# Two of down's four block copies go from VectorE to ScalarE, and tile 14's product is split around the turns of tile 15

## The chip, the cores and the metric

The kernel runs on one core of one Trainium2 chip. The metric is the device time of one launch in microseconds (us), the median of several runs. Its span is the time from the first to the last instruction in a profiled execution.

## The reference

`x` is 64 x 32 x 512 (batch, head, position). First a long convolution per head: a kernel `K` of 512 taps is made from state-space parameters and convolved causally with `x`, masked by a length per batch entry. The result goes through a feed-forward block with ternary weights:

```python
xq = int4_quant(x)                       # round(x * sqrt(7) / mean|x|), clipped to -8..7, rescaled
gate = bitlinear(xq, w_gate, s_gate)     # w_q = clip(round(w / mean|w|), -1, 1)
up = bitlinear(xq, w_up, s_up)
gate = jnp.square(jax.nn.relu(gate))
inter = int8_quant(up * gate)            # round(x * 127 / max|x|)
return bitlinear(inter, w_down, s_down)  # 1376 -> 512
```

The output is `x` plus that. `w_gate` and `w_up` are 1376 x 512, `w_down` is 512 x 1376.

## The kernel before

The 2048 rows are cut into T = 16 tiles of 128 rows (two heads by 64 batch entries). Each engine has its own program, written out by hand, and semaphores tie them together. A loop over slots m = 0..15 runs on every engine; slot m computes the `gate` and `up` products of tile m in three chunks of columns (416, 512, 448; c = 0, 1, 2), and works on other tiles beside them.

TensorE in slot m: `products(m, 0)`, the turns of x for tile m + 4 (`xt`), `products(m, 1)`, `products(m, 2)`, `down` of one or two older tiles (`DOWNS`: none up to slot 4, tile 0 in slot 5, tiles 11 and 12 in slot 14, tile 13 in slot 15), and `conv(m + 4)`. `gate_ps` and `up_ps` have two banks each, so an `up` product waits until the `inter` of two chunks before is made. After slot 15 come `turn_last` (eleven turns of tile 15's rounded `inter` into two PSUM banks), `down(14)` and `last_down`, tile 15's product in two halves of 256 columns.

ScalarE in slot m: `relu_square(c)` for each chunk, two instructions (L780, L783); between them the absolute sum of a later tile (`y_sum`), the copy of the turned x (`xt_copy`), and `y_round(m + 2)` (L745), directly ahead of `relu_square(2)`. It is called by VectorE's `y_scale(m + 2)`. In slot 4 an x load (`load_half(act, 4, 1)`, L347) follows `relu_square(2)`.

VectorE in slot m: `gated(c)` for each chunk, which makes `inter` from `up_ps` and ScalarE's `g2` (L1114) and takes its maximum (L1118); then the row's scale, the rounding of `inter` (L1161), the cast of a turned `inter` (`i_cast`, L1091), the output of older tiles (`out_add`, L1097) and the mask of a `conv` (`y_mask`, L1037). Between `gated(0)` and `gated(1)` stand `q_copy` and `y_scale`.

The weights of down are rounded in slot 2 into `w_int[2]`, turned in four blocks of 128 output columns by DMA transposes that SP issues (`turn_down(0)` and `(1)` in its slot 2, `(2)` and `(3)` in its slot 3, L411) into `dn_turned`, and `down_copy(k)` (L1024) clips block k, 128 x 1408 int16, to -1..1 and writes it as bf16 into `down_t`. VectorE does all four copies in slot 4 (LAG is 5): blocks 0 and 1 ahead of `gated(1)`, blocks 2 and 3 behind it. `down(0)` in slot 5 is the first reader of `down_t`.

At the end VectorE rounds the first 896 columns of tile 15's `inter` and ScalarE the other 480 (L816); both cast the turns. ScalarE also casts tile 14's turned `inter` (L814). `half_add(0)` and `half_add(1)` (L1104) write tile 15's output into `o_sb[1]`, which held tile 13's output, so they wait for tile 13's two stores. SP stores half 0 and ScalarE's queue half 1.

Of the kernel before, what the change touches and what calls it, by code (L numbers as in the profile page):

```python
# [5 lines left out]
P = 128  # L6
ALU = mybir.AluOpType
ACT = mybir.ActivationFunctionType
# [15 lines left out]
def adaln_ffn(nc, x, length, log_dt, C, log_A_real, A_imag, Dskip,  # L24
              w_gate, w_up, w_down, s_gate, s_up, s_down, out):
    B, H, L = x.shape
# [3 lines left out]
    T = B * H // P  # L30
    KB = L // P
    IB = -(-I // P)
# [14 lines left out]
    LAG = 5  # L47
# [8 lines left out]
    with ExitStack() as ctx:  # L56
# [6 lines left out]
        def sem(name):  # L63
            return ctx.enter_context(nc.semaphore(name))

        gate_ps = [psum("gate_ps0"), psum("gate_ps1")]
# [62 lines left out]
        c1 = sb("c1", [P, 2, HG])  # L129
# [95 lines left out]
        w_act_copied = sem("w_act_copied")  # L225
        down_turned = [sem(f"down_turned{k}") for k in range(KB)]
        down_copied = sem("down_copied")

        xt_turned = sem("xt_turned")
        xt_copied = sem("xt_copied")  # L230
# [39 lines left out]
        def half_rows(half):  # L270
            return slice(half * B, (half + 1) * B)
# [79 lines left out]
        def _(sp):  # L351
# [88 lines left out]
            sp.wait_ge(half_ready, 1)  # L440
            for half in range(2):
                sp.dma_start(out[:, head_of(T - 1, half), 0:L // 2],
                             o_sb[1][half_rows(half), 0:L // 2]).then_inc(half_stored[0], 16)
            sp.wait_ge(stored[0], 32 * (T // 2))
            sp.wait_ge(stored[1], 32 * (T // 2 - 1))
            sp.wait_ge(half_stored[0], 32)
# [48 lines left out]
        def _(pe):  # L495
# [25 lines left out]
            def conv(n):  # L521
                pe.wait_ge(xt_copied, n + 1)
                pe.wait_ge(toep_loaded[n % 4], 16 * (n // 4 + 1))
                wait(pe, y_masked, n - 1)
                if n == 1:
                    pe.wait_ge(winv_ready, 2)
                if n == EARLY + 3:
                    pe.wait_ge(k_ready, 3)
                bank = conv_bank(n)
                for i in range(KB):  # L530
                    for half in range(2):
                        mm = pe.matmul(bank[half * B:(half + 1) * B, 0:L - i * P],  # L532
                                       x_t[n % 2][:, i, half * B:(half + 1) * B], toep[n % 4][:, half, i * P:L],
                                       start=(i == 0), stop=(i == KB - 1))
                mm.then_inc(conv_done, 1)
# [85 lines left out]
            def turn_last():  # L621
                pe.wait_ge(inter_quant, T)
                for c in range(IT_SPLIT):
                    mm = pe.transpose(tr_act_ps[:, c * P // 2:(c + 1) * P // 2].bitcast(BF16),
                                      inter_q[:, c * P:(c + 1) * P].bitcast(BF16), ident_bf[:])
                mm.then_inc(it_turned, 1)
                pe.wait_ge(last_quant, 1)
                for c in range(IT_SPLIT, IB):
                    r = P if c < WIDE else IR
                    o = (c - IT_SPLIT) * P // 2  # L630
                    mm = pe.transpose(tr_dve_ps[0:r, o:o + P // 2].bitcast(BF16),
                                      inter_q[:, c * P:c * P + r].bitcast(BF16), ident_bf[:])
                mm.then_inc(it_turned, 1)

            def down(n):
                if n == T - 2:
                    pe.wait_ge(it_act_copied, 1)
                else:
                    pe.wait_ge(it_copied, n + 1)
                if n == 0:  # L640
                    pe.wait_ge(down_copied, KB)
                if n == 8:
                    pe.wait_ge(y_masked, T)
                if down_before(n) is not None:
                    pe.wait_ge(out_ready, down_before(n) + 1)
                bank = down_bank(n)
                for c in range(IB):
                    r = P if c < WIDE else IR
                    mm = pe.matmul(bank[:], i_t[n % 2][0:r, c, :], down_t[0:r, c, :],  # L649
                                   start=(c == 0), stop=(c == IB - 1))  # L650
                mm.then_inc(down_done, 1)

            def last_down():
                pe.wait_ge(it_copied, T - 1)
# [10 lines left out]
            for m in range(T):  # L665
                products(m, 0)
                if m > 0 and m + EARLY < T:
                    xt(m + EARLY)
                products(m, 1)
                if m == 0:  # L670
                    xt(3)
                    conv(2)
                    first_q(1)
                if m == 1:
                    k_sums(2)
                if m == 2:
                    mean(2)
                products(m, 2)
                if m == 0:
                    xt(EARLY)  # L680
                    conv(3)
                for n in DOWNS[m]:
                    if n < T - 2:
                        down(n)
                if m + EARLY < T:
                    conv(m + EARLY)
            turn_last()
            down(T - 2)
            last_down()

        @block.scalar
        def _(act):
# [32 lines left out]
            def weight_copy(i):  # L725
                act.wait_ge(w_turned, i + 1)
                dst, src = inner_blocks(i)
                nc.scalar.activation(dst, src, ACT.Sign).then_inc(w_act_copied, 1)

            def xt_copy(n):  # L730
                act.wait_ge(xt_turned, n + 1)
# [7 lines left out]
            def y_round(n):  # L739
                act.wait_ge(yscale_ready, n + 1)  # L740
                if n >= 4:
                    act.wait_ge(q_loaded[n % 2], 16 * (n // 2 - 1))
                elif n >= 2:
                    act.wait_ge(q_turned, n - 1)
                nc.scalar.activation(y_int[n % 2][:], y[n % 3][:], ACT.Copy, scale=yscale[n % 2][:]  # L745
                                     ).then_inc(y_rounded, 1)
# [27 lines left out]
            for m in range(T):  # L774
                def relu_square(c):
                    cn = CH[c][1]
                    bank = (NC * m + c) % 2
                    act.wait_ge(gate_done, NC * m + c + 1)
                    wait(act, inter_ready, NC * m + c - 1)
                    nc.scalar.activation(g2[bank][:, 0:cn], gate_ps[bank][:, 0:cn], ACT.Relu,  # L780
                                         scale=gu_scale[m % 4][:, 0:1]).then_inc(relu_done, 1)
                    act.wait_ge(relu_done, NC * m + c + 1)
                    nc.scalar.activation(g2[bank][:, 0:cn], g2[bank][:, 0:cn],  # L783
                                         ACT.Square).then_inc(g2_ready, 1)

                relu_square(0)
                if 1 <= m < T - 2:
                    y_sum(m + 2)
                relu_square(1)
                if m == 0:  # L790
                    xt_copy(3)
                    load_half(act, 3, 1)
                    y_sum(2)
                elif m + EARLY < T:
                    xt_copy(m + EARLY)
                if 1 <= m < T - 2:
                    y_round(m + 2)
                relu_square(2)
                if m == 0:
                    y_round(2)  # L800
                    xt_copy(EARLY)
                if m == 4:
                    for i in range(2):
                        act.wait_ge(w_rounded[2][i], rounds(2, i))
                    load_half(act, 4, 1)
                if m < 2:
                    act.wait_ge(w_turned, len(TURNS))
                    weight_sum(2, m)
                if m == 2:
                    down_round(2)  # L810
                    down_round(3)
# [13 lines left out]
            act.wait_ge(half_ready, 2)  # L825
            for half in range(2):
                act.dma_start(out[:, head_of(T - 1, half), L // 2:L],
                              o_sb[1][half_rows(half), L // 2:L]).then_inc(half_stored[1], 16)

        @block.vector  # L830
        def _(dve):
# [268 lines left out]
            def half_add(half):  # L1100
                cols = slice(half * L // 2, (half + 1) * L // 2)
                dve.wait_ge(half_done, half + 1)
                dve.wait_ge(stored[1], 32 * (T // 2 - 1))
                v.scalar_tensor_tensor(out=o_sb[1][:, cols], in0=gate_ps[half][:, 0:L // 2],  # L1104
                                       scalar=oscale[:, T - 1:T], in1=x_tile(T - 1)[:, cols],
                                       op0=ALU.mult, op1=ALU.add).then_inc(half_ready, 1)

            for m in range(T):
# [15 lines left out]
                    q_copy(m + 1)  # L1124
                if 1 <= m < T - 2:
                    y_scale(m + 2)
                if m == LAG - 1:
                    down_copy(0)
                    down_copy(1)
                gated(1)  # L1130
                if m == 0:
                    y_mask(2)
                    q_copy(1)
                    y_scale(2)
                if m == LAG - 1:
                    down_copy(2)
                    down_copy(3)
                if m == 1:
                    k_copy(2)
                    dve.wait_ge(w_turned, len(TURNS))  # L1140
# [70 lines left out]
```

## Time and profile before

| | us |
|---|---|
| timed runs | 209.33, 212.88, 214.0 |
| median | 212.88 |
| the profiled execution, its own time | 208.22 |
| span of the profiled execution | 206.4 |
| TensorE busy in the span | 174.8 |
| VectorE busy | 159.3 |
| ScalarE busy | 114.2 |

The times of the rows below are from the profiled execution, counted from the start of its span. PE is TensorE, DVE is VectorE, ACT is ScalarE, SPq and ACTq are the queues on which SP and ScalarE issue DMAs. The program's names come without their numbers: `inter<-up_ps,gu_scale,g` is L1114. `x4` is the number of instructions merged into one row. `L1114` is line 1114 of the kernel. An entry in brackets at a row's end is how long the engine had been idle before it and what released it. Slot 3 is about 73 to 81 us on TensorE and 77 to 85 us on VectorE, slot 4 81 to 89 and 85 to 95, slot 5 starts at 89 on TensorE.

### The profile page before, as it was taken

How to read it: one execution, taken by the hardware profiler on the slowest of the kernel's cores; microseconds unless marked ns; L12 is line 12 of the kernel's file. 1: busy time of each engine (PE TensorE's matmuls, PEld its weight loads, DVE VectorE, ACT ScalarE, POOL GpSimd, SP SyncE). 2: the span in 40 equal slices, each digit the busy share in tenths (PEclk: the TensorE clock that was granted, in tenths of full speed). 3: DMA queues.
4: the chain of work that ended last, by engine and by line, in shares of the span. 5: the costliest groups of instructions: out<-in, count | busy, mean ns of one | idle time of the engine just before them, and what ended most of it. 6: DMA issues, size and time to landing. Idle time of an engine off the chain costs nothing.

```text
span 206.4 us, 3336 instructions
## 1 busy us (share of the span) xinstructions
PE 174.8 (85%) x1059; PEld 92.7 (45%) x1075; DVE 159.3 (77%) x425; ACT 114.2 (55%) x191; POOL 28.4 (14%) x71
## 2 busy tenths in 40 slices
PE   1003599895999999995999999999999999999982
PEld 1003476652464554452545454545454544444451
DVE  6999495567167898999877787878787989897851
ACT  2363685656478995863382736364554628162720
POOL 5024998950000000000000000000000000000000
PEclk9999999998899999999999999999999999999999
DMA  4999499999934487999575554747471618274424
GB/s 138 362 366 317 74 262 350 398 221 223 191 76 115 97 210 151 243 190 254 153 139 149 111 158 94 176 94 171 99 171 37 122 25 173 44 155 80 92 54 102
DMA packets 49487, 34.25 MB, mean 166 GB/s; under 512 B 37598, under 2 KB 37886, under 8 KB 49470
## 3 DMA queue, kind: packets, MB, share of 16 engines
q1 hardware_dynamic: 45502, 25.65, 54.1%
q10 hardware_dynamic: 3968, 8.39, 13.1%
q8 instruction: 9, 0.15, 0.3%
q14 instruction: 8, 0.07, 0.1%
HBM read 21.07 MB, written 4.28 MB: 123 GB/s over the span
## 4 chain that ended last, share of the span: by engine, by line
PE 66%; DMA 14%; DVE 9%; ACT 4%; issue 3%; POOL 1%; SPq 1%; DVEq 0%; POOLq 0%; ACTq 0%
PE gate_ps L612 14%; PE up_ps L617 13%; PE down_ps L649 11%; DMA raw<-in_L_ffn_w_up_dram 8%; PE conv_ps L532 6%; PE tr_dve_ps L532 6%; DMA raw<-in_x_dram 5%; PE conv_ps L649 5%; PE down_ps L532 4%; PE tr_act_ps L518 3%; DVE inter L1114 2%; ACT int L710 2%; DVE y L1037 1%; DVE imax L1118 1%; ACT g L780 1%
## 5 line engine op out<-in xcount | busy, mean ns | idle before, releaser
L780 ACT ACTIVATE g<-gate_ps,gu_scale 128x416 f32<-128x416 f32 (+2 forms) x48 | 30.6, 637 | 52.9 <-PE gate_ps L612 52.6
L1114 DVE SCALAR_TENSOR_TENSOR inter<-up_ps,gu_scale,g 128x416 f32<-128x416 f32 (+2 forms) x48 | 33.3, 693 | 20.9 <-ACT g L783 20.6
L617 PE MATMUL up_ps<-up_t,q_t 128*128 128x512 bf16 (+2 forms) x190 | 44.6, 357 | 2.9 <-DVE inter L1114 2.8
L612 PE MATMUL gate_ps<-gate_t,q_t 128*128 128x448 bf16 (+2 forms) x181 | 42.8, 356 | 0.6
L1118 DVE TENSOR_REDUCE imax<-inter 128x1 f32<-128x416 f32 (+2 forms) x48 | 30.3, 631 | 1.7
L783 ACT ACTIVATE g<-g 128x416 f32<-128x416 f32 (+2 forms) x48 | 28.1, 585 | 1.5
L617 PEld LDWEIGHTS up_ps<-up_t,q_t 128*128 128x128 bf16 x192 | 18.5, 98 | 21.9 <-DVE inter L1114 4.1
L649 PE MATMUL down_ps<-down_t,i_t 128*128 128x512 bf16 (+1 forms) x119 | 27.7, 379 | 0.1
L612 PEld LDWEIGHTS gate_ps<-gate_t,q_t 128*128 128x128 bf16 x192 | 17.7, 98 | 16.0 <-issue 2.1
L710 ACT ACTIVATE int<-raw 128x2048 bf16<-128x2048 f32 (+3 forms) x8 | 15.6, 1944 | 9.3 <-DMA raw<-in_L_ffn_w_gate_dram 5.2
L532 PE MATMUL conv_ps<-toep,x_t 128*64 128x512 f32 (+3 forms) x128 | 19.0, 439 | 0.0
L649 PEld LDWEIGHTS down_ps<-down_t,i_t 128*128 128x128 bf16 (+1 forms) x121 | 11.8, 98 | 13.7
L745 ACT ACTIVATE y_int<-y,yscale 128x512 int16<-128x512 f32 x16 | 11.5, 721 | 6.0 <-DVE yscale L1045 5.7
L1161 DVE TENSOR_SCALAR inter_q<-inter,iscale 128x1376 int16<-128x1376 f32 x15 | 14.0, 936 | 0.5
L532 PEld LDWEIGHTS conv_ps<-toep,x_t 128*64 128x64 f32 x128 | 8.7, 136 | 11.2 <-issue 9.8
L737 ACT ACTIVATE y_abs<-y 128x512 bf16<-128x512 f32 x16 | 9.9, 616 | 5.5 <-DVE y L1037 5.5
L509 PE MATMUL down_ps<-wsum,averaging 128*128 128x3 f32 (+1 forms) x6 | 1.5, 312 | 12.9 <-ACT int L710 12.9
L532 PE MATMUL tr_dve_ps<-toep,x_t 128*64 128x512 f32 (+3 forms) x80 | 11.9, 439 | 0.0
L733 ACT COPY x_t<-tr_act_ps 128x512 f32<-128x512 f32 x16 | 9.2, 574 | 3.5 <-PE tr_act_ps L518 3.5
L649 PE MATMUL conv_ps<-down_t,i_t 128*128 128x512 bf16 (+1 forms) x44 | 10.2, 379 | 0.0
L518 PE MATMUL tr_act_ps<-ident,raw 128*128 128x128 f32 x48 | 7.7, 285 | 2.2 <-DMA raw<-in_x_dram 2.2
L1037 DVE SCALAR_TENSOR_TENSOR y<-steps,lens,conv_ps 128x512 f32<-128x512 f32 x8 | 5.9, 742 | 3.7 <-PE conv_ps L532 3.7
(179 smaller groups left out, 206.0 us busy)
## 6 DMA issues: line engine op xcount, KB each, us to landing
toep<-k_back SPq DMA_DIRECT2D x16, 512.0 KB, 4.1
out_dram<-o_sb SPq DMA_DIRECT2D x30, 128.0 KB, 2.4
raw<-in_x_dram ACTq DMA_DIRECT2D x3, 512.0 KB, 8.5
raw<-in_x_dram SPq DMA_DIRECT2D x3, 512.0 KB, 9.5
raw<-in_L_ffn_w_down_dram ACTq DMA_DIRECT2D x1, 1472.0 KB, 14.7
raw<-in_L_ffn_w_down_dram ACTq DMA_DIRECT2D x1, 1280.0 KB, 9.4
raw<-in_L_ffn_w_gate_dram ACTq DMA_DIRECT2D x1, 1024.0 KB, 5.6
raw<-in_L_ffn_w_gate_dram SPq DMA_DIRECT2D x1, 1024.0 KB, 10.4
```

Source lines behind the costliest of these rows:

```text
L518: mm = pe.transpose(tr_act_ps[:, i * P:(i + 1) * P], x_tile(n)[:, i * P:(i + 1) * P], ident[:])
L532: mm = pe.matmul(bank[half * B:(half + 1) * B, 0:L - i * P], x_t[n % 2][:, i, half * B:(half + 1) * B], toep[n % 4][:, half, i * P:L], sta ...
L612: mm = pe.matmul(gate_ps[bank][:, 0:cn], q_t[m % 3][:, i, :], gate_t[:, i, c0:c0 + cn], start=(i == 0), stop=(i == KB - 1))
L617: mm = pe.matmul(up_ps[bank][:, 0:cn], q_t[m % 3][:, i, :], up_t[:, i, c0:c0 + cn], start=(i == 0), stop=(i == KB - 1))
L649: mm = pe.matmul(bank[:], i_t[n % 2][0:r, c, :], down_t[0:r, c, :], start=(c == 0), stop=(c == IB - 1))
L710: nc.scalar.activation(w_bits[m][weight_part(m, i)], raw[m][weight_part(m, i)], ACT.Abs, accum_out=wsum[:, m, i:i + 1]).then_inc(w_summed, 1)
L745: nc.scalar.activation(y_int[n % 2][:], y[n % 3][:], ACT.Copy, scale=yscale[n % 2][:]).then_inc(y_rounded, 1)
L780: nc.scalar.activation(g2[bank][:, 0:cn], gate_ps[bank][:, 0:cn], ACT.Relu, scale=gu_scale[m % 4][:, 0:1]).then_inc(relu_done, 1)
L783: nc.scalar.activation(g2[bank][:, 0:cn], g2[bank][:, 0:cn], ACT.Square).then_inc(g2_ready, 1)
L1114: v.scalar_tensor_tensor(out=inter[:, c0:c0 + cn], in0=up_ps[bank][:, 0:cn], scalar=gu_scale[m % 4][:, 1:2], in1=g2[bank][:, 0:cn], op0=AL ...
L1118: return v.tensor_reduce(imax[:, c:c + 1], inter[:, c0:c0 + cn], AX.X, ALU.max, apply_absolute_value=True)
L1161: v.tensor_scalar(inter_q[:, 0:I], inter[:], iscale[:], None, ALU.mult).then_inc(inter_quant, 1)
```

## The change

Block 1 of down is copied by ScalarE in slot 3 and block 3 by ScalarE in slot 4, each between `y_round` and `relu_square(2)`, by an activation `Sign` (the values are whole numbers, so it is the clip). VectorE copies block 0 in slot 3 and block 2 in slot 4, both between `gated(1)` and `gated(2)`. `down(0)` waits for two copies of each engine. `down(14)` is cut: its first four matmuls stand ahead of `turn_last`, the other seven behind it. Tile 15's output goes into the first 512 columns of `inter` instead of `o_sb[1]`, and `half_add` no longer waits for tile 13's stores.

```diff
+        down_act_copied = sem("down_act_copied")
             for half in range(2):
                 sp.dma_start(out[:, head_of(T - 1, half), 0:L // 2],
-                             o_sb[1][half_rows(half), 0:L // 2]).then_inc(half_stored[0], 16)
+                             inter[half_rows(half), 0:L // 2]).then_inc(half_stored[0], 16)
...
-            def down(n):
+            def down(n, c0=0, c1=IB):
...
                 if n == 0:
-                    pe.wait_ge(down_copied, KB)
+                    pe.wait_ge(down_copied, KB // 2)
+                    pe.wait_ge(down_act_copied, KB // 2)
...
-                for c in range(IB):
+                for c in range(c0, c1):
...
-                mm.then_inc(down_done, 1)
+                if c1 == IB:
+                    mm.then_inc(down_done, 1)
...
+            down(T - 2, 0, 4)
             turn_last()
-            down(T - 2)
+            down(T - 2, 4)
             last_down()
...
+            def down_copy(k):
+                act.wait_ge(down_turned[k], 16)
+                nc.scalar.activation(down_t[:, :, k * P:(k + 1) * P], dn_turned[:, k],
+                                     ACT.Sign).then_inc(down_act_copied, 1)
...
                 if 1 <= m < T - 2:
                     y_round(m + 2)
+                if m in (3, 4):
+                    down_copy(2 * m - 5)
                 relu_square(2)
...
                 act.dma_start(out[:, head_of(T - 1, half), L // 2:L],
-                              o_sb[1][half_rows(half), L // 2:L]).then_inc(half_stored[1], 16)
+                              inter[half_rows(half), L // 2:L]).then_inc(half_stored[1], 16)
...
                 dve.wait_ge(half_done, half + 1)
-                dve.wait_ge(stored[1], 32 * (T // 2 - 1))
-                v.scalar_tensor_tensor(out=o_sb[1][:, cols], in0=gate_ps[half][:, 0:L // 2],
+                v.scalar_tensor_tensor(out=inter[:, cols], in0=gate_ps[half][:, 0:L // 2],
...
-                if m == LAG - 1:
-                    down_copy(0)
-                    down_copy(1)
                 gated(1)
...
-                if m == LAG - 1:
-                    down_copy(2)
-                    down_copy(3)
+                if m in (3, 4):
+                    down_copy(2 * m - 6)
```

## Rows read from the trace of the kernel before

**Rows 1.** Windows of core 0: stretch, busy time (instructions) per engine, granted clock, DMA share.

```profile
50.00:54.00 4.00, 4.00 (x16) 1.71 (x17) 1.32 (x4) 2.91 (x3) 0.00 (x0) 0.59 1.40 195
95.83:100.00 4.17, 4.17 (x21) 1.75 (x23) 3.52 (x9) 1.82 (x3) 0.00 (x0) 1.00 0.92 168
100.00:196.00 96.00, 95.47 (x507) 46.77 (x513) 79.14 (x180) 49.91 (x91) 0.00 (x0) 1.00 0.52 118
```

**Rows 2.** Timeline of TensorE: start, length, instruction, [idle before and its releaser].

```profile
49.80 1.08 PE L518 MATMUL tr_act_ps<-ident,raw 128*128 128x128 f32 x4 [2.23 <-DMA raw<-in_x_dram]
50.81 3.58 PE L532 MATMUL down_ps<-toep,x_t 128*64 128x512 f32 x16
54.34 2.37 PE L532 MATMUL conv_ps<-toep,x_t 128*64 128x512 f32 x16
...
91.85 1.04 PE L617 MATMUL up_ps<-up_t,q_t 128*128 128x512 bf16 x4 [0.17 <-DVE inter L1114]
...
95.83 0.93 PE L617 MATMUL up_ps<-up_t,q_t 128*128 128x448 bf16 x4 [2.18 <-DVE inter L1114]
```

**Rows 3.** Chain that ended last, 86 to 91 us: start, length, what.

```profile
86.66 1.58 DVE down_t L1024 x2
...
90.33 0.88 DVE down_t L1024
```

**Rows 4.** Timeline of all engines, 194 to 203 us.

```profile
194.05 1.35 ACT L814 CAST i_t<-raw 128x1408 bf16<-128x1408 int16 x1
...
196.99 0.56 PE L624 MATMUL tr_act_ps<-ident_bf,inter_q 128*128 128x128 bf16 x7 [0.99 <-DVE inter_q L1165]
...
201.90 0.48 DVE L1104 SCALAR_TENSOR_TENSOR o_sb<-gate_ps,oscale,raw 128x256 f32<-128x256 f32 x1 [0.95 <-DMA out_dram<-o_sb]
...
202.60 0.48 DVE L1104 SCALAR_TENSOR_TENSOR o_sb<-gate_ps,oscale,raw 128x256 f32<-128x256 f32 x1 [0.22 <-PE gate_ps L661]
```

**Rows 5.** Chain that ended last, 197 to 203 us.

```profile
197.78 2.38 PE conv_ps L649 x11
200.16 2.42 PE gate_ps L661 x22
```

**Rows 6.** Instructions of line 728: count, shortest/median/longest ns, first and last start.

```profile
L728 ACT ACTIVATE gate_t<-up_ps x2: 1005/1009/1013, 28.6 to 35.4; 128x1024 bf16<-128x1024 int16 x2
```

**Rows 7.** Timeline of slots 3 and 4, VectorE, ScalarE and its queue.

```profile
79.33 0.72 ACT L745 ACTIVATE y_int<-y,yscale 128x512 int16<-128x512 f32 x1 [1.19 <-DVE yscale L1045]
...
79.96 0.62 ACT L780 ACTIVATE g<-gate_ps,gu_scale 128x448 f32<-128x448 f32 x1
79.98 0.69 DVE L1118 TENSOR_REDUCE imax<-inter 128x1 f32<-128x512 f32 x1
...
81.22 0.69 DVE L1114 SCALAR_TENSOR_TENSOR inter<-up_ps,gu_scale,g 128x448 f32<-128x448 f32 x1 [0.56 <-ACT g L783]
...
84.80 0.65 DVE L1114 SCALAR_TENSOR_TENSOR inter<-up_ps,gu_scale,g 128x416 f32<-128x416 f32 x1
...
86.70 0.72 ACT L745 ACTIVATE y_int<-y,yscale 128x512 int16<-128x512 f32 x1 [0.64 <-DVE yscale L1045]
...
88.03 0.63 ACTq L347 DMA_DIRECT2D raw<-in_x_dram  x1
...
91.12 0.68 DVE L1114 SCALAR_TENSOR_TENSOR inter<-up_ps,gu_scale,g 128x448 f32<-128x448 f32 x1
```

**Rows 8.** Line 411 by halves; then landing times of down's blocks 1, 2 and 3.

```profile
L411 SPq DMA_TRANSPOSE int<-int x2: 1747/1938/2128, 73.1 to 75.3; - x2
...
L411 SPq DMA_TRANSPOSE int<-int x2: 1392/2224/3056, 82.0 to 83.4; - x2
...
int<-int SPq DMA_TRANSPOSE x1, 4.0
...
int<-int SPq DMA_TRANSPOSE x1, 4.8
...
int<-int SPq DMA_TRANSPOSE x1, 6.2
```

## The prediction

> **What bounds the kernel now.** I read the windows first, because they say where TensorE has room. From 100 to 196 us it is busy for 95.47 of 96 us at full granted clock [rows 1]: nothing that happens on another engine there can move the end, and what TensorE loses before 100 us it never gets back. So two places count: what delays TensorE before that stretch, the four copies of down's turned blocks among it, and the tail behind 196 us.
>
> TensorE's own timeline shows its pauses in slots 4 and 5. The last `up` product of slot 5 starts at 95.83 after 2.18 us idle, the one before it at 91.85 after 0.17 us [rows 2]. Both wait for `inter` (L1114) on VectorE, since `up_ps` has two banks. Read next the chain of waits ahead of that product: `down_copy` stands on it, with 1.58 us for its first two and 0.88 us for its last [rows 3]. VectorE is the bound of slot 4, the four copies being 3.2 us of it (4 x 0.79).
>
> The tail is a line of dependent work: the seven turns of tile 15 begin at 196.99 after TensorE stood idle 0.99 us for VectorE's rounding, then come tile 14's eleven matmuls (2.38 us) and the 22 half matmuls (2.42 us) [rows 4, 5], `half_add(1)` at 202.60 [rows 4], and the last two stores, issued by ScalarE's queue.
>
> **The tail, part by part.** Four of tile 14's eleven matmuls move ahead of the turns: 4 x 2.38 / 11 = 0.87 us. They need `i_t[0]`, which ScalarE's cast gives at 194.05 + 1.35 = 195.40 [rows 4], and the output of tile 12 added, which VectorE does ahead of all its work of slot 15. TensorE falls idle at 196.00 and is called at 196.99, so 0.87 fits into 0.99 us, with 0.12 us over; bound of the price if the pipeline is slower to drain: 0 to 0.1 us. Behind the turns only 7 x 0.216 = 1.51 us remain, and they still cover the casts of tile 15: the turns end at 197.78 and the seven matmuls at 199.29, while the casts, of 896 columns and of 480, can't take longer than the 1.35 us of the 1408 above, which is 199.1. The half matmuls start 0.87 us earlier, at 199.29, and end at 201.71; `half_add(1)` starts at about 201.73 instead of 202.60.
>
> That only holds because of the buffer. Today `half_add(0)` waits 0.95 us for the store of tile 13 and starts at 201.90; it costs nothing, since `half_add(1)` waits for TensorE 0.22 us more after it [rows 4]. With the split alone, that store would still hold `half_add(0)` until 201.90 and `half_add(1)` would follow at 202.31, so the split would bring 0.3 us. With `inter` as target the wait is gone: `half_add(0)` can go at 199.29 + 1.21 = 200.5 plus the matmul's drain, in time behind tile 14's addition, which can start at 199.3. The two parts together give 0.87 us; all DMAs behind (SP's two for half 0, ScalarE's two for half 1) keep their number and size and move forward. `inter` is free: its last readers are the two roundings that the turns wait for. Bounds: 0.77 to 0.87 us gained.
>
> **The copies, part by part.** VectorE loses the four copies of slot 4 and gets one back in slot 3 and one in slot 4; one of its copies takes 0.88 us, 0.79 from start to start [rows 3]. ScalarE gets one in each slot. No `Sign` of this size is in the trace. Its cast of the same 1408 columns took 1.35 us [rows 4]; a `Sign` of 1024 columns out of PSUM took 1.01 us [rows 6], which scaled is 1.39. I take 1.35, or 1.26 from start to start, because instructions on ScalarE overlap by 0.09 us (`y_int` at 79.33 lasts 0.72 and its follower starts at 79.96 [rows 7]); bounds 1.2 and 1.4.
>
> What matters is where ScalarE's copy stands: between `y_round` and `relu_square(2)`, and `gated(2)` on VectorE waits for the latter. In slot 3 that is already the late side: `y_int` starts at 79.33, `gated(2)` at 81.22, after VectorE waited 0.56 us for ScalarE [rows 7]. So `gated(2)` goes to 81.22 + 1.26 = 82.48. VectorE's own copy is hidden there: `imax` at 79.98 ends at 80.67, the copy at 81.5. Price of slot 3: 1.26 us. Block 1, which ScalarE copies, is there: issued at 75.3, landed 4.0 us later [rows 8], 79.3, before ScalarE reaches it at 79.96.
>
> From `gated(2)` of slot 3 to `gated(0)` of slot 4 VectorE works without a stop, 84.80 - 81.22 = 3.58 us; new: 86.06. From there to slot 4's `y_int` 86.70 - 84.80 = 1.90 us [rows 7]: 87.96. Then ScalarE: the 1.89 us that slot 3 shows from `y_int` to `gated(2)`, and 1.26 for its copy, would let `gated(2)` start at 91.11. It started at 91.12 [rows 7]. So with all data there, what VectorE is rid of in slot 4 (three copies, 2.4 us) is spent exactly: ScalarE's copies stand on the path one after the other, and slots 3 and 4 together come out at nil. `gated(1)` and block 2's copy on VectorE (landed at 82.0 + 4.8 = 86.8 [rows 8]) end near 90.1 and are hidden.
>
> But block 3 is late. Its transpose is issued at 83.4 and lands 6.2 us later, at 89.6 [rows 8]. Before, `down_copy(3)` stood at 90.33 and did not see that. Now ScalarE would begin at 87.96 + 0.63 = 88.6 and waits 1.0 us, with `relu_square(2)` and the x load of the last quad queued behind it. SP issues the transpose behind the same things as before: its order is unchanged, and the `y_round` of slot 3 that it follows comes ahead of the first copy. So I keep 89.6. `gated(2)` of slot 4 starts at 92.15, 1.03 us later than now; VectorE works on without a stop to `gated(0)` of slot 5, which releases the product of 95.83. That product starts at 96.9. Bounds: with block 3 landed within the 4.0 us of block 1 (87.4) nil; with 7 us (90.4), +1.8.
>
> ScalarE's x load is issued at 88.03 today [rows 7], while block 3 is on its way. The Trainium skill (DMA: Bandwidth & Descriptors, section "Issuing engines are not separate DMA queues") says that DMAs of all issuing engines share the same 16 engines and interleave. By this rule the x load, now queued behind the copy, would leave block 3's last 1.6 us alone, and block 3 would land earlier by up to 1 us: the sum would be that of rival (a). No row of the trace shows a transpose with and without a load beside it, so it neither agrees nor disagrees.
>
> **The sum**, against the profiled execution (208.22 us, of which 206.4 span): -0.87 in the tail, +1.03 in slots 3 and 4 = +0.16 us, 208.4. The timed runs of before are 209.33, 212.88 and 214.0, and all four shown scatter over 5.8 us, far more than the change. Their middle is 211.1 with the profiled one and 212.88 without; I put the new median between, at 212.0 + 0.2 = 212.2 us. Two per cent, 4.3 us, is about what a measurement of this kernel can tell from no change.
>
> **Rivals.** (a) Block 3 lands by 88.6: slots 3 and 4 come out at nil, the tail's 0.87 us stands alone: profiled 207.35, median 211.2. For it: blocks 1 and 2 took 4.0 and 4.8 us. Against: SP's issue of one of the last two took 3.06 us where another took 1.39 [rows 8], and what stands in that queue is unchanged.
>
> (b) ScalarE has room and its copies cost nothing, as its many waits for TensorE suggest. Then slot 3 costs 0.23 us (VectorE's copy past its 0.56 us pause) and slot 4 gains 2.4: -2.1, within the 2.35 us of pauses in [rows 2], and -3.0 with the tail: profiled 205.2, median 209.1. Against: its waits lie before `relu_square(0)`, not between `y_round` and `relu_square(2)`, where the copy is.
>
> (c) Slower: TensorE's clock falls. Behind a pause of 2.23 us before 49.80 the granted clock was 0.59 from 50 to 54 us, and `conv` took 3.58 us instead of 2.37; after the 2.18 us before 95.83 it stayed at 1.00 [rows 1, 2]. Two pauses alike, and one was followed by the lower level of 1.2 and 2.4 GHz. Now TensorE waits for `gated(0)` in slot 4 (1.1 us), for `gated(2)` in slot 5 (1.0) and again about 2.2 us. If the clock falls, the 4 us behind the pause lose the 1.2 us of `conv` and, as an estimate, half as much again in what runs ahead of it: +1.8 on top of +0.16, profiled 210.2, median 214.0. It decides once block 3 lands later than about 89.6, which lengthens the pause. The Trainium skill (TensorE: Matmul & The Clock Gate, Part 1) says that an idle stretch takes the clock down; the trace agrees at the first pause and shows at the second that not every one does it.
>
> **Chances.** Forecast 0.48, (a) 0.22, (b) 0.08, (c) 0.14, something unseen 0.08. None reaches 2% by itself; the scatter of the runs can: faster 0.06, same 0.88, slower 0.06. The range: from (b) with a little of the scatter, 208.5, to (c) likewise, 214.7; the forecast's own is 209.3 to 214.
>
> **What would show it.** In the trace after: ScalarE's `Sign` of 1408 columns near 80.0 lasting 1.35 us; `gated(2)` of slot 3 near 82.5; the second `Sign` starting at 89.6 with ScalarE idle 1 us before it, released by a DMA; the last `up` product of slot 5 near 96.9 instead of 95.83; four matmuls of tile 14 between 195.8 and 197; no DMA ahead of the first `half_add`; and 4.7 us instead of 5.6 from the first turn of tile 15 to `half_add(1)`. A second `Sign` without idle time before it makes the forecast wrong on the gain's side, a granted clock under 1.00 from 96 to 101 us on the other.

## The result

Before 210.26 us (median of 20 runs, 208.8 to 214.0), after 208.64 us (median of 20, 207.73 to 210.31). The ratio is 0.9936, 95% interval 0.9913 to 0.996: 1.35 us faster, between 0.84 and 1.83 (the ratio leaves out runs more than 1.5% above the fastest of their kernel; the medians of all runs differ by 1.62). The forecast was 212.2 us, from a sum of 0.16 us slower; the sign was wrong. Of the 3.6 us between 212.2 and 208.64, 1.7 are the base: it put before at 212.0 from four runs, and 20 runs give 210.26. The scatter that it feared stayed in the single runs: with 20 of them the interval is 0.24% to either side.

The profiled executions hide it. Their own times are 208.22 before and 208.26 after, their spans 206.4 and 206.5. So the first thing to do is to take both in stretches that begin and end at the same instructions. Timeline of TensorE in the kernel after (the numbers in brackets are idle time before the row, and its releaser):

```profile
51.01 1.01 PE L519 MATMUL tr_act_ps<-ident,raw 128*128 128x128 f32 x4 [2.61 <-DMA raw<-in_x_dram]
51.95 3.66 PE L533 MATMUL down_ps<-toep,x_t 128*64 128x512 f32 x16
...
79.20 0.93 PE L618 MATMUL up_ps<-up_t,q_t 128*128 128x448 bf16 x4 [0.44 <-DVE inter L1124]
...
87.82 0.93 PE L618 MATMUL up_ps<-up_t,q_t 128*128 128x448 bf16 x4 [0.96 <-DVE inter L1124]
...
96.89 0.93 PE L618 MATMUL up_ps<-up_t,q_t 128*128 128x448 bf16 x4 [1.39 <-DVE inter L1124]
```

Two more rows of TensorE's timeline in the kernel before, slot 3's last `up` product and the first product of slot 6:

```profile
78.14 0.93 PE L617 MATMUL up_ps<-up_t,q_t 128*128 128x448 bf16 x4 [0.43 <-DVE inter L1114]
...
101.37 0.88 PE L612 MATMUL gate_ps<-gate_t,q_t 128*128 128x416 bf16 x4
```

Against [rows 2]: the turns of x behind the load start at 51.01 instead of 49.80, and slot 5's last `up` product at 96.89 instead of 95.83. This execution is 1.06 us late before any changed instruction runs: slot 3's last `up` product, the one ahead of all the edits, starts at 79.20 here and at 78.14 in before. From that product to slot 5's last one it is 96.89 - 79.20 = 17.69 us here and 95.83 - 78.14 = 17.69 us there. The copies' move came out at nil, to 0.01 us. The pauses of TensorE are the same sum in other places: 0.96 + 1.39 here, 0.17 + 2.18 in [rows 2].

ScalarE and VectorE in slots 3 and 4, after, beside [rows 7]:

```profile
80.39 0.72 ACT L754 ACTIVATE y_int<-y,yscale 128x512 int16<-128x512 f32 x1 [1.19 <-DVE yscale L1056]
...
81.02 1.36 ACT L736 ACTIVATE down_t<-int 128x1408 bf16<-128x1408 int16 x1
...
83.54 0.68 DVE L1124 SCALAR_TENSOR_TENSOR inter<-up_ps,gu_scale,g 128x448 f32<-128x448 f32 x1 [1.02 <-ACT g L792]
...
87.12 0.64 DVE L1124 SCALAR_TENSOR_TENSOR inter<-up_ps,gu_scale,g 128x416 f32<-128x416 f32 x1
...
89.01 0.72 ACT L754 ACTIVATE y_int<-y,yscale 128x512 int16<-128x512 f32 x1 [1.91 <-DVE yscale L1056]
...
89.64 1.36 ACT L736 ACTIVATE down_t<-int 128x1408 bf16<-128x1408 int16 x1
...
92.17 0.68 DVE L1124 SCALAR_TENSOR_TENSOR inter<-up_ps,gu_scale,g 128x448 f32<-128x448 f32 x1 [1.02 <-ACT g L792]
```

The `Sign` takes 1.36 us. From `y_int` to `gated(2)` it is 3.15 us in slot 3 (1.89 in [rows 7]: 1.26 more), and 3.16 in slot 4. The second `Sign` has no idle time before it: block 3 was there. Its transpose was issued at 84.4 and landed after 4.7 us, at 89.1, where [rows 8] have 6.2. Issue and landing in the kernel after:

```profile
L412 SPq DMA_TRANSPOSE int<-int x2: 1391/2079/2767, 83.0 to 84.4; - x2
...
int<-int SPq DMA_TRANSPOSE x1, 4.7
```

The chain that ended last runs through both `Sign`s, one behind the other, where it ran through VectorE's copies in [rows 3]:

```profile
80.35 0.66 DVE inter L1124
81.02 1.36 ACT down_t L736
82.38 0.53 ACT g L789
...
89.64 1.36 ACT down_t L736
91.00 0.53 ACT g L789
```

The tail after, beside [rows 4, 5]:

```profile
196.89 1.03 PE L651 MATMUL conv_ps<-down_t,i_t 128*128 128x512 bf16 x4
...
198.05 0.56 PE L625 MATMUL tr_act_ps<-ident_bf,inter_q 128*128 128x128 bf16 x7
...
198.68 1.68 PE L651 MATMUL conv_ps<-down_t,i_t 128*128 128x512 bf16 x7
...
201.60 0.48 DVE L1114 SCALAR_TENSOR_TENSOR inter<-gate_ps,oscale,raw 128x256 f32<-128x256 f32 x1 [0.45 <-PE gate_ps L664]
...
202.80 0.48 DVE L1114 SCALAR_TENSOR_TENSOR inter<-gate_ps,oscale,raw 128x256 f32<-128x256 f32 x1 [0.72 <-PE gate_ps L664]
```

Four matmuls fill the pause, and the turns' row has no idle time in brackets. From the first turn to the second half's addition: 202.80 - 198.05 = 4.75 us, against 202.60 - 196.99 = 5.61 in [rows 4]. The gain is 0.86 us. The first addition is released by TensorE, no longer by a DMA. From slot 3's last `up` product to the end of the span it is 206.5 - 79.20 = 127.3 us here and 206.4 - 78.14 = 128.3 in before: 1.0 us less, the tail's 0.86 and 0.1 behind the second addition. In this execution that is offset by the 1.06 us that it was late before.

### The profile page after: what moved, and what is told of

Its sections match the earlier page's. It is cut to its first block, busy times and chain, and to the rows that moved or that the text cites. A ratio compares the mean times of both kernels' runs of the same rounds, so it can differ in the third digit from the quotient of the medians.

```text
span 206.5 us, 3335 instructions
## 1 busy us (share of the span) xinstructions
PE 174.9 (85%) x1059; PEld 92.8 (45%) x1075; DVE 157.8 (76%) x423; ACT 116.6 (56%) x193; POOL 28.0 (14%) x71
## 4 chain that ended last, share of the span: by engine, by line
PE 65%; DMA 14%; DVE 10%; ACT 5%; issue 3%; POOL 1%; SPq 1%; DVEq 0%; POOLq 0%
PE up_ps L618 14%; PE gate_ps L613 13%; PE down_ps L651 11%; DMA raw<-in_L_ffn_w_up_dram 8%; DMA raw<-in_x_dram 6%; PE conv_ps L533 6%; PE tr_dve_ps L533 4%; PE conv_ps L651 4%; PE down_ps L533 4%; DVE inter L1124 3%; PE tr_act_ps L519 3%; ACT int L714 2%; DVE imax L1128 2%; DVE y L1048 1%; ACT down_t L736 1%
```

## The experiments

Theory A, from these two traces: the whole gain is the tail's 0.86 us, and the copies are worth nil because ScalarE's two stand whole on the path. It leaves 0.5 us of the measured 1.35 unexplained (0.4 with what lies behind the second addition), which its interval allows. Theory B: the copies bring those 0.5 us in some way that these two profiles don't show. The recorded forecast: block 3 is late and the copies cost 1.03 us.

**e1, the tail alone.** Both tail edits on the kernel before:

```diff
-            down(T - 2)
+            down(T - 2, 0, 4); turn_last(); down(T - 2, 4)
-  o_sb[1] in half_add and its two stores, with the wait on stored[1]
+  inter
```

> The kernel before with the tail's two edits alone (product of tile 14 split 4 and 7, last output in the intermediate's buffer), the copies all on VectorE. Theory A, which follows from the trace after: the whole gain is the tail's, 0.87 us, and the copies come out at nil; then this gives 0.87 us less than before, ratio near 0.996, and 4.75 us instead of 5.61 from the first turn of tile 15 to the second half's addition. Theory B: the copies bring the rest of the measured 1.35 us, about 0.5; then this still gives 0.87 us. A tail that brings more than 0.9 us, or none, would fell both.

Measured: ratio 0.9932 (0.9891 to 0.9974). In its profile 197.99 to 202.74, 4.75 us. The ratio is 0.04 points from that of the whole change: the tail alone gives what the change gives, within the intervals. By the ratio that is 1.4 us, more than the 0.9 at which both theories were to fall, but its interval (0.5 to 2.3 us) holds the 0.86. That speaks for A, since what exceeds 0.86 us shows up here without the shared copies; it doesn't prove it.

**e2, the split alone**, with the last output in `o_sb[1]` as before.

> The split of tile 14's product alone, the last output still in the buffer of tile 13's output. By the prediction's working the store of tile 13 holds the first half's addition, so the split brings only about 0.3 us: the first addition starts where it did and waits some 1.8 us for a DMA, the second follows 0.4 us behind it. Rival: the wait for the store is not late without the other edit, then the split brings the full 0.87 us.

Measured: 0.9979 (0.994 to 1.0017). VectorE's timeline in e2, both additions in one row:

```profile
204.77 0.88 DVE L1106 SCALAR_TENSOR_TENSOR o_sb<-gate_ps,oscale,raw 128x256 f32<-128x256 f32 x2 [2.04 <-DMA out_dram<-o_sb]
```

The first turn is at 199.65, the second addition starts 0.88 - 0.48 = 0.40 us behind the first, at 205.17: 5.52 us, 0.09 us less than before where 0.3 was worked out. The store landed 5.12 us behind the first turn and not 4.91 as before. The mechanism is as predicted: without the other buffer the split is nearly worthless, since 2.04 us of DMA wait stand in its place.

**e8, the buffer alone**, the product of tile 14 whole.

> The kernel before with the last output in the intermediate's buffer and no other edit. By the prediction's working nothing: the first half's addition starts about 0.4 us earlier, the second still waits for TensorE at 5.6 us from the first turn of tile 15. Ratio 1.000. Rival: the earlier stores of half 0 shorten the end by themselves, up to 0.5 us.

Measured: 1.0022 (0.9984 to 1.006). In its profile the turns start at 199.75, the additions at 204.16 and 205.36: 5.61 us to the second, as before. So the two tail edits are worth 0.1 and 0 us by themselves and 0.86 together.

**e3, the copies alone**, the tail as before.

> The copies' move alone, the tail as before. Theory A: nil (ratio 1.000), from the last product of slot 3 to the last up product of slot 5 17.7 us as before, and block 3 landed before ScalarE comes to it. The recorded forecast: block 3 lands late, 1.03 us slower, ratio 1.005, with about 1 us of ScalarE idle for a DMA ahead of the second copy. Theory B: 0.5 us faster, ratio 0.998.

Measured: 0.997 (0.9935 to 1.0005). Slot 3's to slot 5's last `up` product: 97.56 - 79.89 = 17.67 us. The second `Sign` has no idle time before it:

```profile
90.33 1.36 ACT L734 ACTIVATE down_t<-int 128x1408 bf16<-128x1408 int16 x1
```

No loss of 1.03 us (1.005 lies outside the interval): the forecast's step is refuted. Nil and half a microsecond of gain both lie inside.

**e6, the cost of a copy doubled.** ScalarE copies block 1 twice.

```diff
+                if k == 1:
+                    nc.scalar.activation(down_t[:, :, k * P:(k + 1) * P], dn_turned[:, k],
+                                         ACT.Sign).then_inc(copied_once, 1)
+                    act.wait_ge(copied_once, 1)
```

> The changed kernel with ScalarE's copy of block 1 done twice, one after the other, in slot 3. Theory A (ScalarE's copies stand whole on the path to slot 5's last up product): 1.3 to 1.5 us slower than the changed kernel, ratio to before near 1.000. If a copy there is covered by ScalarE's pauses: no difference, 0.994.

Measured: 1.0015 (0.9978 to 1.0052), and 99.63 - 80.53 = 19.10 us in its profile, 1.41 more than 17.69 (one `Sign` and the wait for it, 1.39 from start to start). VectorE's pause before `gated(2)` of slot 3 grows from 1.02 to 2.44 us. A copy there costs its whole length. By the ratios it is 1.7 us slower than the changed kernel, which the intervals can't tell from 1.4.

**e4, the copies in another place.** Behind `relu_square(2)`, where ScalarE waited for TensorE, instead of ahead of it.

```diff
-                if m in (3, 4):
-                    down_copy(2 * m - 5)
                 relu_square(2)
+                if m in (3, 4):
+                    down_copy(2 * m - 5)
```

> The changed kernel with ScalarE's two copies behind the third chunk's two activations in slots 3 and 4 instead of ahead of them, where ScalarE waits about 1.0 us for TensorE. If it is the place of the copies that eats VectorE's relief (theory A), the product that starts late in slot 5 starts about 2.1 us earlier, and the kernel takes 2.1 us less than the changed one: ratio to before near 0.986. If ScalarE's copies cost the same wherever they stand, it equals the changed kernel, 0.994.

Measured: 0.9863 (0.981 to 0.9917), 207.11 us. In the profile:

```profile
78.64 0.93 PE L618 MATMUL up_ps<-up_t,q_t 128*128 128x448 bf16 x4 [0.43 <-DVE inter L1124]
...
94.22 0.93 PE L618 MATMUL up_ps<-up_t,q_t 128*128 128x448 bf16 x4 [0.41 <-DVE inter L1124]
```

94.22 - 78.64 = 15.58 us, 2.11 less than 17.69. It is the number of rival (b) of the prediction, to 0.1 us: the relief of VectorE is real, and the place of ScalarE's copies ate it. Not all of it reaches the end: from slot 3's last `up` product to the end of the span it is 204.1 - 78.64 = 125.5 us against 127.3 in after, 1.8 less, and by the ratios the kernel is 1.5 us faster than the changed one, with an interval that holds 2.1 as well. `gated(2)` of slot 3 comes right behind VectorE's own copy. Here ScalarE does wait for block 3, and that costs little (in e10 below, without this wait, the 15.58 us are 15.45):

```profile
90.20 1.38 ACT L736 ACTIVATE down_t<-int 128x1408 bf16<-128x1408 int16 x1 [1.02 <-DMA int<-int]
```

**e7, block 3 made late.** SP issues it behind tile 3's transpose.

```diff
                 if m in (2, 3):
                     turn_down(2 * m - 4)
-                    turn_down(2 * m - 3)
+                if m == 2:
+                    turn_down(1)
...  (m == 4, behind the transpose of inter_q)
+                        turn_down(3)
```

> The changed kernel with block 3's transpose issued behind the transpose of tile 3's intermediate instead of ahead of it, some 3.6 us later, so that it lands about 3 us after ScalarE comes to it. The recorded prediction's pricing: every microsecond of landing past that point costs one, so about 3.1 us slower than the changed kernel, ratio to before near 1.009. Its rival (c): the longer pause of TensorE in slot 5 is followed by a lower granted clock, 1.2 to 1.8 us more, near 1.016. If VectorE or TensorE have room for a late landing, less than 2 us.

Measured: 1.0071 (1.0027 to 1.0115). The block was issued at 88.62 and landed 5.1 us later.

```profile
93.78 1.38 ACT L739 ACTIVATE down_t<-int 128x1408 bf16<-128x1408 int16 x1 [3.42 <-DMA int<-int]
...
97.06 1.67 PE L621 MATMUL up_ps<-up_t,q_t 128*128 128x512 bf16 x4 [0.21 <-DVE inter L1127]
98.52 1.70 PE L616 MATMUL gate_ps<-gate_t,q_t 128*128 128x448 bf16 x4
101.04 0.93 PE L621 MATMUL up_ps<-up_t,q_t 128*128 128x448 bf16 x4 [0.82 <-DVE inter L1127]
```

ScalarE waits 3.42 us, slot 5's last product comes at 101.04 - 79.82 = 21.22 us, 3.53 us later than 17.69. So the prediction's price, a microsecond for each that the block is late, is right in this profile; in the timed runs it is 2.8 us over the changed kernel by the ratios, nearer the 3.1 that was expected than nil. The clock fell too (0.57 from 97 to 101 us; the two products in the fence took 1.67 and 1.70 instead of 1.03 and 0.92), but TensorE still had 0.82 us to wait behind them: rival (c) happened and cost nothing in this execution.

**Why block 3's landing differs** was then the open question. It took 6.2 us in the profile before, 6.1 in e1, 4.7 in after and 4.6 in e3, 6.3 in e4. Two candidates: a transpose of y that SP issues some 5 us behind it, and the transpose of tile 3's `inter` right behind it.

**e5**, e4 with tile 6's transpose of y held back:

```diff
                 sp.wait_ge(y_rounded, n + 1)
+                if n == 6:
+                    sp.wait_ge(down_turned[3], 16)
```

> The kernel with ScalarE's copies behind the third chunk, and SP holding tile 6's transpose of y back until block 3 of down has landed. In three traces block 3 took 6.1 to 6.3 us to land and tile 6's transpose had been issued 4.9 to 5.1 us after it; in two others it took 4.7 to 4.8 us and that transpose came 5.3 us or later. Theory Q: the two transposes meet on the DMA engines, and block 3 now lands after 4.7 us, so ScalarE's wait of 1.0 us for it is gone; the last up product of slot 5 starts up to 0.3 us earlier. Theory R: block 3's landing varies by itself, or with the transpose of tile 3 issued right behind it; then it still takes 6.1 us or more here. Ratio to before 0.986 to 0.984.

Measured: 0.9843 (0.9795 to 0.9891). Landing 6.1 us, ScalarE's wait 0.92 us. Theory Q falls. Block 2 was late too, 6.6 us from issue, and VectorE waited 0.41 us for it.

**e11**, e4 with the transpose of tile 3's `inter` held back:

```diff
                     sp.wait_ge(inter_quant, m)
+                    if m == 4:
+                        sp.wait_ge(down_turned[3], 16)
```

> The kernel with ScalarE's copies behind the third chunk, and SP holding back the transpose of tile 3's intermediate until block 3 of down has landed. Theory I: that transpose, issued at the very end of block 3's issue, is what stretches block 3's landing from 4.7 to 6.2 us; then it lands after 4.7 to 4.9 us here. Theory R: the landing is long for another reason and stays at 6 us. VectorE waits for that transpose ahead of tile 4's rounding, so the time itself may be up to 1 us longer.

Measured, a single run: 214.0 us. Block 3 took 6.2 us to land and block 2 6.7, and theory I falls as well. The hold cost far more than I wrote: the transpose of tile 3 was issued at 90.53, and everything behind it in SP's queue with it; TensorE stood idle 5.61 us before slot 5's last `up` product, and the clock was 0.50 from 100 to 104 us.

**e10 and e12, the pause in slot 0.** e10 and e4 have the same DMAs, and only TensorE's program differs: unread matmuls in the wait for x, which takes a pause of 1.84 to 3.60 us in the profiles of all kernels but e12, with a clock of 0.50 to 0.81 from 50 to 54 us in every one of them. (The text on record for e10 says 2.2 us or more; e5 had 1.84 and e8 1.98.)

```diff
                 if m == 0:
+                    pe.wait_ge(y_masked, 2)
+                    fill(8)        # e12: fill(15); each a 128x512 matmul into down_ps, never read
                     xt(EARLY)
```

> The kernel with ScalarE's copies behind the third chunk, and the same eight unread matmuls in TensorE's wait for x in slot 0, ahead of which every profile has a pause of 2.2 us or more and behind it a clock of 0.50 to 0.81 from 50 to 54 us. If that pause brings the clock down: clock 1.00 there, conv in 2.3 us instead of 3.5, the turns of x in 0.5 instead of 1.0, and 1.2 to 1.7 us less than without the filling, ratio to before near 0.979. If not: 0.986 as without it.

Measured, e10: 0.9839 (0.9809 to 0.9868), 206.18 us. In the profiled execution the filling was too short: x landed so late that the pause was still 2.42 us, and the clock was 0.78 and then 0.80. In the other five runs the mean clock was 0.997 to 1.000, where no run of e4 was over 0.992. But its block 3 landed in time, with ScalarE's copy at 89.65 and no idle time ahead of it:

```profile
89.65 1.36 ACT L742 ACTIVATE down_t<-int 128x1408 bf16<-128x1408 int16 x1
```

The same DMA program gave a wait of 1.02 us in e4 and none in e10.

> The kernel with ScalarE's copies behind the third chunk, with fifteen unread matmuls (15 x 0.216 = 3.2 us) in TensorE's wait for x in slot 0. With eight of them the pause in the profile was still 2.42 us, since x landed 4.1 us after the last product, and the clock was 0.78 and 0.80 from 50 to 58 us. With fifteen the pause is 0 to 1.2 us. If pauses bring the clock down: 1.00 from 50 to 58 us, conv in 2.3 us, mean clock of the runs 0.997 or more, and 1.2 to 1.7 us less than without filling, ratio to before near 0.979. If the clock there follows from something else: 0.98 to 0.986, and conv still 3 us or longer. Where x lands early, the filling itself costs up to 0.3 us.

Measured, e12: 0.9789 (0.9754 to 0.9824), 206.08 us. Windows and timeline of e12:

```profile
50.00:54.00 4.00, 3.95 (x24) 1.99 (x24) 2.15 (x7) 1.79 (x2) 0.00 (x0) 1.00 1.45 218
54.00:58.00 4.00, 3.46 (x28) 1.82 (x25) 1.32 (x2) 1.12 (x2) 0.00 (x0) 1.00 0.87 186
```

```profile
51.57 0.60 PE L519 MATMUL tr_act_ps<-ident,raw 128*128 128x128 f32 x4
52.10 2.37 PE L533 MATMUL down_ps<-toep,x_t 128*64 128x512 f32 x16
```

The clock stays at 1.00, `conv` takes 2.37 us instead of 3.58 [rows 2]. From the turns of x to slot 3's last `up` product it is 78.82 - 51.57 = 27.25 us, against 78.64 - 50.29 = 28.35 in e4: the filling is worth 1.1 us where the clock would fall. The kernel is 2.1% under before and faster than the changed one. In the timed runs the filling's own part is not shown: against e4 it is 1.0 us by the medians, but the intervals overlap, and e10 (eight matmuls, 206.18 us) and e5 (none, 206.51 us) are as close to 206.08. The filling computes nothing that is used.

Block 3 took 6.0 us to land here, and ScalarE waited 0.75 us for it, with e4's DMA program again. All profiles together:

| ScalarE's copies | block 3, us from issue to landing |
|---|---|
| none, all four on VectorE in slot 4 | before 6.2, e1 6.1, e2 6.1, e8 5.8, e9 6.2 |
| ahead of `relu_square(2)`, as in the change | after 4.7, e3 4.6, e6 4.7 |
| behind `relu_square(2)` | e4 6.3, e5 6.1, e10 4.5, e11 6.2, e12 6.0 |

e10 against e4 and e12 shows that one DMA program can give either. But all three profiles with the change's order are short and all five of the order before are long, so it isn't shown that the landing is independent of the kernel. In each of the nine profiles with 5.8 us or more, the DMA traffic of this core falls to 40 GB/s or less for 0.75 to 1.45 us at a stretch before block 3 lands, and then goes on at about 290. In after, e3 and e10 no such stretch of 0.25 us or longer lies before the landing; in e6 the last 0.55 us are one. (e7 issues block 3 later than the others: 5.1 us, with such a stretch of 1.35.) GB/s in steps of 0.05 us over the last 2 us before the landing, e4 (88.2 to 90.2) and e10 (87.2 to 89.2):

```profile
GB/s 97 184 251 195 225 225 200 220 236 169 189 154 102 36 15 0 0 0 0 0 0 5 5 10 10 20 10 20 15 10 5 10 15 31 261 271 297 282 297 282
...
GB/s 292 287 287 287 282 307 282 205 36 108 282 292 292 287 292 287 297 282 292 282 302 292 287 297 262 84 15 61 72 148 220 210 184 241 220 205 215 225 169 225
```

In such a stretch the core's other transfers hardly move anything either, so that time wasn't lost to them. Why the traffic stops isn't found.

**e9, the same in slot 5 of the kernel before.** It was to settle what the half microsecond of theory B is. The e8 profile had the same pause of 2.19 us in slot 5 as [rows 2], but the clock fell behind it:

```profile
97.00:101.00 4.00, 4.00 (x12) 1.62 (x13) 3.34 (x9) 1.82 (x3) 0.00 (x0) 0.59 1.09 203
```

```profile
96.98 1.68 PE L617 MATMUL up_ps<-up_t,q_t 128*128 128x448 bf16 x4 [2.19 <-DVE inter L1113]
98.45 3.44 PE L649 MATMUL down_ps<-down_t,i_t 128*128 128x512 bf16 x11
```

From there to slot 6 it took 104.12 - 96.98 = 7.14 us, where before took 101.37 - 95.83 = 5.54: 1.6 us. The shared copies cut that pause into 0.96 and 1.39 us, so they could save this where it happens.

```diff
                 mm.then_inc(gate_done, 1)
+                if (m, c) == (5, 2):
+                    fill(8)
```

> The kernel before, with eight matmuls of 128x512 whose result nobody reads (8 x 0.216 = 1.7 us) in TensorE's pause of 2.2 us in slot 5. Theory C: in the kernels with all copies on VectorE the granted clock falls behind that pause in part of the runs (in one profile to 0.59, 1.6 us lost), and about half of their runs have a mean clock under 0.987, against a fifth with shared copies; that would be the part of the measured gain that the tail doesn't explain. Then here only about a fifth of the runs are under 0.987, and the mean time is 0.3 to 0.5 us lower than before, ratio about 0.998; the profile has the last up product of slot 5 where before has it. If the low clock comes from elsewhere, half the runs stay under 0.987 and the ratio is 1.000.

Measured: 1.0007 (0.997 to 1.0045), and 6 of 12 runs still under 0.987. In its profile the pause is 0.46 us and slot 5's last product is where it was (96.59 - 78.91 = 17.68). Theory C isn't borne out: taking that pause away gave nothing that can be measured. The difference in the mean clocks that it started from is there all the same: under 0.987 are 9 of 44 runs of the kernels with the copies shared as in the change (after, e3, e6) and 19 of 36 of those with all copies on VectorE and no filling (e1, e2, e8). Where it comes from is open.

## Why the prediction was wrong

**The step that failed is block 3's landing.** "So I keep 89.6": I took the landing of one execution of the kernel before, 6.2 us, for the changed kernel, because SP's order was unchanged, and built +1.03 us on it. The changed kernel's block 3 landed after 4.7 us, in e3 after 4.6 and in e6 after 4.7, each time before ScalarE came to it, so ScalarE's wait was nil and not 1.0 us. An unchanged order of issue doesn't fix the landing: with the same DMA program it made ScalarE wait 1.02 us in e4 and not at all in e10. With block 3 in time the prediction's own working gives nil for the copies, and nil is what the trace shows, 17.69 us against 17.69. The sum becomes rival (a), 0.87 us gained, to which I had given 0.22. The second miss is the base of the median, 212.0 us for a kernel that takes 210.26.

**The working beside it held.** The price of the copy (1.35 taken, 1.36 measured), its place on the path (1.26 us in slot 3; 1.41 for one more in e6), the balance of slots 3 and 4, and the price of lateness (3.53 us for 3.42 us of waiting in e7) came out to a tenth of a microsecond in the profiles.

**The tail held** in all its parts: 0.87 forecast, 0.86 measured, in after and in e1 alike; the matmuls fit into the pause. That the split needs the buffer held too; only its worth alone was 0.1 and not 0.3 us, because tile 13's store landed 0.2 us later behind the turns.

**Rival (b)** was argued away rightly for this change, and its number, 2.1 us, is what the same two copies bring 1.2 us further down ScalarE's program (e4). **Rival (c)**: the clock does fall behind some such pauses, at 1.6 us in e8, but not in the changed kernel's profile.

**The x load** of ScalarE's queue did move behind block 3's landing in after (issued at 91.62), and by the Trainium skill's rule on shared engines (DMA: Bandwidth & Descriptors, "Issuing engines are not separate DMA queues") that was to give rival (a)'s sum, which came. But the load isn't needed for a long landing: in e4 it was issued at 90.27, behind the landing, which still took 6.3 us. No run moved the load alone, so what it did in the kernel before isn't shown, and that the sum came out by this rule may be luck.

**What stays open.** The measured 1.35 us is 0.4 to 0.5 more than the trace shows. The interval (0.84 to 1.83) holds the 0.86, and e1 alone measures as much as the whole change, so nothing more need be there. Kernels with shared copies had a low mean clock in fewer runs; e9 speaks against the pause in slot 5 as the reason, and no run shows that this is part of the gain. And what decides between a landing of 4.7 and of 6.2 us isn't found, nor whether the change itself made it short: with either neighbouring transpose held back (e5, e11), or with the x load behind it (e4), it still took 6 us and more.

## What to carry to other kernels

Moving work from the engine that bounds a stage to one that waits a lot pays only where the other engine waits: ask what is next in its program and who waits for that. Here the same two copies are worth nil ahead of one pair of activations and 2.1 us behind it (1.5 by the timed runs). A landing time read from one execution of one kernel is no constant of the next: where the sum's sign hangs on it, take the rows of all transfers of its kind and give the cases like chances. Where two edits clear the same spot, a pause and the store behind it, try them one at a time before you judge either: each alone gave at most 0.1 us, both 0.86.

## What the runs showed of the hardware

Executions of one DMA program differed by over 1 us in when a DMA transpose of 128 x 1408 landed (4.5 us from issue in e10, 6.3 in e4), and in the nine profiles where it took 5.8 us or more, the core's DMA traffic had almost stopped for 0.75 to 1.45 us before. A pause of TensorE of 2.2 us in the midst of dense products was followed by the full clock in three profiles (before, e1, e2) and by a lower one in two: 0.59 in e8, with 1.6 us lost, and 0.57 in e7; behind 5.61 us (e11) it was 0.50. Fifteen unread matmuls in a wait of about 3 us kept it at 1.00 and `conv` at 2.37 us. The Trainium skill (TensorE: Matmul & The Clock Gate, Part 1) says that an idle stretch lowers the clock; the traces agree behind the wait for x, and behind the shorter pauses in slot 5 in two of five. Two profiles can agree within 0.1 us of span while the kernels differ by 1.35 us in the timed runs, because x landed 1.2 us later in one of them.
